# The down projection of the shared experts: one fp32 matmul on raw operands in place of three matmuls on rounded parts

## The reference

```python
def _L0_ffn_ref(x, w12, w3, router_w, expert_bias, sw1, sw2, sw3):
    g = x @ sw1.T                       # 1024 shared hidden channels
    u = x @ sw2.T
    shared_out = jax.nn.silu(g) * u @ sw3.T
    scores = jax.nn.sigmoid(x @ router_w.T)
    _, top_idx = jax.lax.top_k(scores + expert_bias, 2)     # 2 of 8 routed experts
    ...                                 # routed experts: 128 hidden channels each
    return shared_out + routed_out
```

## Time and profile before

| | us |
|---|---|
| median of 3 runs | 1803.8 (1801.58 to 1804.18) |
| the profiled execution's own time | 1802.2 |
| its span, first to last instruction | 1800.1 |
| PE busy | 1553.0 (86% of the span) |
| DVE busy | 1184.8 (66%) |
| ACT busy | 894.5 (50%) |
| mean granted TensorE clock | 0.929 of full speed |

### The profile page before, as it was taken

The page is one execution under the profiler, slowest core; times in us unless marked ns, Lnnn a source line. Parts: engine busy times, 40 slices in busy tenths (PEclk is TensorE's granted clock), DMA queues, the critical chain, the costliest instruction groups (busy, mean ns, idle before and its releaser), DMA issues. The chain is left out here.

```text
span 1800.1 us, 26927 instructions
## 1 busy us (share of the span) xinstructions
PE 1553.0 (86%) x8952; PEld 1190.4 (66%) x8958; DVE 1184.8 (66%) x2139; ACT 894.5 (50%) x2156; POOL 585.7 (33%) x688
## 2 busy tenths in 40 slices
PE   5899799889987884917699999999999999999492
PEld 4444488668863333817488888888888888888372
DVE  4666463676358996356377877778777877777632
ACT  2356444234435551415366666666666666665241
POOL 3110233312344652448322232222332223320163
PEclk9899899889987996958699999999999999999796
DMA  3320144214410005740000000000000000000463
GB/s 76 61 43 13 57 141 112 74 55 142 110 48 0 1 0 182 147 148 13 1 13 1 24 1 13 13 13 13 11 15 1 25 1 13 1 1 1 164 142 110
DMA packets 62053, 89.95 MB, mean 50 GB/s; under 512 B 10192, under 2 KB 44240, under 8 KB 61920
## 3 DMA queue, kind: packets, MB, share of 16 engines
q1 hardware_dynamic: 53664, 65.68, 11.9%
q0 software_dynamic: 8256, 22.56, 5.8%
HBM read 62.38 MB, written 19.40 MB: 45 GB/s over the span
## 5 line engine op out<-in xcount | busy, mean ns | idle before, releaser
L1375 DVE TENSOR_REDUCE gqa_neg_max<-acc 128x1 f32<-128x1024 f32 (+7 forms) x256 | 193.4, 755 | 176.4 <-PE acc L1484 175.2
L1261 ACT ACTIVATE gqa_probsT_high<-aux 128x512 fp32r<-128x512 f32 x288 | 172.0, 597 | 249.5 <-PE aux L1492 248.7
L1380 DVE TENSOR_TENSOR gqa_probsT_low<-aux,gqa_probsT_high 128x512 fp32r<-128x512 f32 x288 | 198.2, 688 | 29.8 <-ACT gqa_probsT_high L1261 25.5
L1270 ACT ACTIVATE gqa_probs<-acc,gqa_neg_max 128x1024 f32<-128x1024 f32 (+7 forms) x256 | 189.3, 739 | 31.4 <-DVE gqa_neg_max L1375 26.3
L1492 PE MATMUL aux<-ident,gqa_probs 128*128 128x128 f32 x1152 | 174.4, 274 | 0.0
L504 POOL DMA_INDIRECT f_xs<-tokens,f_slot_token x108 | 106.8, 989 | 140.8 <-DVE f_slot_token L670 84.2
L1503 PE MATMUL aux<-gqa_probsT_high,gqa_v_high 128*128 128x512 f32 x288 | 146.6, 509 | 1.0 <-DVE gqa_probsT_low L1380 1.0
L1168 POOL TENSOR_SCALAR gqa_q_scale<-gqa_q_scale 128x4 f32<-128x4 f32 x64 | 16.3, 255 | 383.3 <-ACT gqa_square L1205 383.0
L1515 PE MATMUL aux<-gqa_wo,gqa_oT 128*128 128x256 f32 x512 | 132.4, 381 | 4.4 <-DVE stream L1368 3.5
L1482 PE MATMUL acc<-gqa_k_high,gqa_q_low 128*128 128x512 f32 (+5 forms) x384 | 132.8, 346 | 0.0
L1482 PE MATMUL acc<-gqa_k_low,gqa_q_high 128*128 128x512 f32 (+5 forms) x384 | 132.7, 346 | 0.0
(11 more groups left out here) (401 smaller groups left out, 3951.4 us busy)
## 6 DMA issues: line engine op xcount, KB each, us to landing
outputs_by_slot<-f_y_tile SPq DMA_DIRECT2D x108, 128.0 KB
f_ws<-in_f_up SPq DMA_DIRECT2D x48, 256.0 KB, 4.2
f_ws<-in_f_down SPq DMA_DIRECT2D x48, 128.0 KB, 4.3
mat_qk<-mat_high SPq DMA_DIRECT2D x64, 64.0 KB, 2.3
f_w<-in_f_up SPq DMA_DIRECT2D x16, 256.0 KB, 4.4
tokens<-f_ln_xn SPq DMA_DIRECT2D x4, 1024.0 KB, 6.1
gqa_w_q<-in_g_wq SPq DMA_DIRECT2D x8, 512.0 KB, 3.5
gqa_wo<-in_g_wo SPq DMA_DIRECT2D x8, 512.0 KB, 3.8
```

The costliest lines, as they stand in the source:

```text
L1261: act.activation(probsT_high[:, u % RING, :], aux[:, u % 2, :], ACT.Copy).then_inc(cell_high_ready, 1)
L1270: act.activation(out, scores(n), ACT.Exp, bias=neg_max[:, j % (2 * JOBS):j % (2 * JOBS) + 1], accum_out=row_sum[:, n // 2 % 4, m, n % 2:n ...
L1375: dve.tensor_reduce(neg_max[:, j % (2 * JOBS):j % (2 * JOBS) + 1], scores(n), AXY, ALU.max, negate=True).then_inc(max_ready, 1)
L1380: dve.tensor_tensor(probsT_low[:, u % RING, :], aux[:, u % 2, :], probsT_high[:, u % RING, :].bitcast(F32), ALU.subtract).then_inc(cell_lo ...
```

## The change

For the shared experts the down projection uses the raw fp32 hidden values and the raw fp32 down weights. The parts `round` go away on ACT and on DVE, and with them `high`, `low` and their semaphores. `split` works on the 512 up columns only. The down weights have buffers of their own (`w_down`, four slots): those of experts 0 to 3 are loaded where they were loaded before, and those of experts 4 to 7 after all other loads in SP's list, each behind a wait for the down steps that free its slot. `down` waits for `hidden` and for its weights. `hide` waits for the down step that read its buffer, four steps earlier.

```diff
             if i == 3:
-                steps.extend([("round", 0), ("place", 0)])
+                steps.append(("place", 0))
             elif i == 4:
-                steps.extend([("invert", 0), ("round", 1), ("round", 2), ("down", 1), ("round", 3)])
-            elif i > 4 and i != FRONT:
-                steps.append(("round", i - 1))
+                steps.extend([("invert", 0), ("down", 1)])
...
-            w = sb("w", [P, STAGES, UP + D])
+            w = sb("w", [P, STAGES, UP])
+            w_down = sb("w_down", [P, SLOTS, D])
...
-            w_high = sb("w_high", [P, SLOTS, UP + D], F32R)
-            w_low = sb("w_low", [P, SLOTS, UP + D], F32R)
+            w_high = sb("w_high", [P, SLOTS, UP], F32R)
+            w_low = sb("w_low", [P, SLOTS, UP], F32R)
...
-            high = sb("high", [P, SLOTS, HALF], F32R)
-            low = sb("low", [P, SLOTS, HALF], F32R)
...
-                sp.dma_start(w[:, m % STAGES, UP:], down_dram[e:e + 1].rearrange("a p n -> (a p) n")).then_inc(w_in[m % STAGES], 16)
+                if e < SLOTS:
+                    sp.dma_start(w_down[:, e, :], down_dram[e:e + 1].rearrange("a p n -> (a p) n")).then_inc(down_in[e], 16)
+
+            for e in range(SLOTS, shared):
+                sp.wait_ge(down_done, 2 * (e - SLOTS) + 2)
+                sp.dma_start(w_down[:, e % SLOTS, :], down_dram[e:e + 1].rearrange("a p n -> (a p) n")).then_inc(down_in[e % SLOTS], 16)
...
-                act.wait_ge(w_in[m % STAGES], 32 * (m // STAGES) + 32)
+                act.wait_ge(w_in[m % STAGES], 16 * (m // STAGES) + 16)
...
                 if n >= HIDDEN:
-                    dve.wait_ge(low_ready, n - HIDDEN + 1)
+                    dve.wait_ge(down_done, n - HIDDEN + 1)
...
-                pe.wait_ge(low_ready, n + 1)
+                pe.wait_ge(hidden_ready, n + 1)
+                if n % 2 == 0:
+                    pe.wait_ge(down_in[s], 16 * (n // 2 // SLOTS) + 16)
...
-                    for a, b in three(high[:, n % SLOTS, cols], low[:, n % SLOTS, cols], w_high[:, s, UP:], w_low[:, s, UP:]):
-                        last = pe.matmul(acc[:, tile // 2, tile % 2 * D:(tile % 2 + 1) * D], a, b,
-                                         start=False, stop=False, skip_group_check=True)
+                    last = pe.matmul(acc[:, tile // 2, tile % 2 * D:(tile % 2 + 1) * D], hidden[:, n % HIDDEN, cols], w_down[:, s, :],
+                                     start=False, stop=False, skip_group_check=True)
```

More of the change, by code:

```diff
@@ L282, in sparse @@
                 steps.extend([("turn", s), ("part", s)])
-            if shared and s == 0:
-                steps.append(("round", FRONT - 1))
             if shared and s < 2:
@@ L305, in order @@
             dense(i)
-        steps.append(("round", 2 * shared - 1))
         steps.extend([("down", 2 * shared - 2), ("down", 2 * shared - 1)])
@@ L401, in ffn_layer @@
         w_in = [sem(f"w_in{r}") for r in range(STAGES)]
+        down_in = [sem(f"down_in{r}") for r in range(SLOTS)]
         w_high_ready = sem("w_high_ready")
@@ L408, in ffn_layer @@
         hidden_ready = sem("hidden_ready")
-        high_ready = sem("high_ready")
-        low_ready = sem("low_ready")
         down_done = sem("down_done")
@@ L556, in _ @@
                     silu(n)
[L557 to L561, removed]
                 elif kind == "part":
@@ L707, in _ @@
                     shares()
[L708 to L711, removed]
                 elif kind == "part" and not PLAIN:
```

## The result

The changed kernel took 1809.24 us (median of 10 runs, 1805.2 to 1813.01) against 1800.35 us (10 runs, 1795.57 to 1804.18) for the kernel before. The medians are 8.9 us apart; the ratio of the runs, which is not that of the two medians, is 1.0041, with a 95% interval of 1.0027 to 1.0055. By this interval it is slower by 4.9 to 9.9 us. The forecast was 1809.5 us, in a range of 1804 to 1815, and a difference of +6.7 us. That the time hits so closely is partly luck, since further runs of the kernel before came out lower than the three known then. A second timing gave 1.0036 (1.0022 to 1.0050), with medians 5.2 us apart.

What follows compares the result with a forecast made beforehand. PE's list of matmuls was taken to bound the two shared layers; dearer down steps +9.6, ended waits -2.2 and smaller splits -0.7 made +6.7 us, forecast 1809.5 us, range 1804 to 1815.

Steps and rivals of the forecast that it cites:

- PE is the bound: In both shared layers PE hardly pauses, so their length is PE's list of matmuls and the change is priced there.
- The price of a step: Each of 32 down steps goes from 1.42 to 1.72 us, eight fp32 records of 0.215 us: +9.6 us.
- The rule of four passes for three: At the down steps, a true fp32 product takes four passes: 1.90 us, +0.47 us a step, +15 us in all.
- The waits that go: PE's waits for rounded hidden before down(0), down(1), down(7) and down(15) end: 1.1 us a layer, -2.2 us.
- The smaller splits: Shorter splits on ACT and DVE are almost all unneeded cover: -0.7 us, bounds 0 and -1.4.
- in two places: Shorter splits reach PE only at the second layer's start, -0.3 us, and before up(2), together -0.4 us.
- What is moved: Four late down-weight loads per layer, last in SP's list, and hide's new wait for down(n-4) cost nothing.
- The sum: Whole kernel: +9.6 - 2.2 - 0.7 = +6.7 us, forecast 1809.5 us.
- The swallowing rival: PE's pauses in the shared layers vanish, gaining 6.2 us; net +3.4 us, 1805.6 to 1807.2 us; chance 0.11.
- The clock: PE's granted clock is 1.00 behind the first layer's head; falling below 1.00 there would show the prediction wrong.

Runs made afterwards that it cites:

- Doubling the step: The changed kernel with each down matmul issued twice; 1861.14 us.
- reordering: The kernel before with its three-part down step and only the order of roundings, splits and the last token tile's addition changed; ratio 0.9978, median 1798.24 us.
- The run with one part: The kernel before with only the product of the two rounded parts in down, four matmuls a step in place of twelve; 1787.6 us.
- the rounding kept: The changed kernel with the rounding kept on ACT and DVE, its results unread, and down made to wait for it; 1808.38 us.
- The run with only the matmul changed: The kernel before with down on raw operands; wide splits, rounding and waits for it stay; ratio 1.0055, median 1810.24 us.
- the run with wide splits: The changed kernel with all splits but the first widened again to 768 columns, the last 256 of them zeros; 1812.78 us.

## Why the prediction was right

*PE is the bound.* Right, within limits. Doubling the step and reordering moved the time by what PE's list says. The run with one part shows the limit: a fall of 0.95 us a step is paid out only by half.

*The price of a step.* Right in mechanism, a little high in size: 0.215 us a record, as the sparse tiles had it, but the step differs by 0.288 us and not 0.30, so +9.2 us in place of +9.6; the 0.30 came from single starts rounded against the change. The rule of four passes for three, from the Trainium skill (FP8 and Floating Point Precision, section TensorE Precision Notes), would make the ratio of the steps 1.33 if a pass cost what a part costs. No trace here agrees with that ratio: the steps stand at 1.71 / 1.42 = 1.20, and the measurement decides.

*The waits that go.* Predicted 0.33, 0.23, 0.32 and 0.24 us a layer; the gains of A, B, C and E are 0.36, 0.41, 0.31 and 0.21. Only B is clearly off. There two clearing matmuls stand ahead of `down(1)`, and the first of them waits for DVE's cast of the slots. The 0.64 us in the earlier trace rows are not that wait: the first clearing matmul has no record in that trace. The second trace of the kernel before has both, and a wait of 0.42 us. There DVE comes to the cast from a split:

```profile
249.90 0.95 DVE L586 TENSOR_TENSOR f_w_low<-f_w,f_w_high 128x768 fp32r<-128x768 f32 x1
250.76 0.17 DVE L670 CAST f_slot_token<-acc 128x23 uint32<-128x23 f32 x1
...
250.99 0.61 PE L918 MATMUL acc<-zeros 128*128 128x512 bf16 x2 [0.42 <-DVE f_slot_token L670]
```

In the changed kernel the wait is 0.28 us, since DVE is early and waits for the turn-over itself, 2.46 us:

```profile
247.73 0.18 DVE L663 CAST f_slot_token<-acc 128x23 uint32<-128x23 f32 x1 [2.46 <-PE acc L895]
...
247.97 0.60 PE L908 MATMUL acc<-zeros 128*128 128x512 bf16 x2 [0.28 <-DVE f_slot_token L663]
248.41 3.62 PE L776 MATMUL acc<-f_w_down,f_hidden 128*128 128x256 f32 x16
```

The prediction had not counted these 0.14 us; with its 0.23 they make 0.37 of the 0.41. The missing rounding is not what brings them. With the rounding kept DVE is early as well, and the second clearing matmul stands 249.94 - 249.26 = 0.68 us behind the last matmul of the turn-over, as in the changed kernel; in the kernel before it was 0.82 in both traces (in the first, 245.53 less 244.71). In the kernel before:

```profile
244.71 0.17 PE L905 MATMUL acc<-f_in_tile_start,f_in_row 128*128 128x23 bf16 x1
```

With the rounding kept (this trace lacks the record of the first clearing matmul too, so the 0.50 us are not all wait):

```profile
249.26 0.17 PE L913 MATMUL acc<-f_in_tile_start,f_in_row 128*128 128x23 bf16 x1
249.47 0.18 DVE L677 CAST f_slot_token<-acc 128x23 uint32<-128x23 f32 x1 [0.34 <-PE acc L913]
...
249.94 0.38 PE L926 MATMUL acc<-zeros 128*128 128x512 bf16 x1 [0.50 <-DVE f_slot_token L677]
```

The run with only the matmul changed has 0.67. So the longer `down(0)`, which puts the turn-over later, is what covers DVE here; the 0.26 us that the kept rounding adds in B are the wait before `down(1)` itself. For C and E the gain was right and the reason too narrow: longer steps cover these two waits even where the rounding stays.

*The smaller splits.* This is the step that failed, by its sentence that they reach PE "in two places". The term was put at 0.7 us, with a bound of 1.4; by the traces it is 2 x 0.47 + 0.3 + 0.3 = 1.5. The start of the second layer came as described: PE now waits for L601's successor, L594, and the first router matmul starts 3.18 us after the first transposes, where it took 3.51. At `up(2)` of the second layer 0.27 us went (0.91 to 0.64 from the first ranking matmul to the second matmul of `up(2)`), as priced. The second layer of the run with the rounding kept has 0.64 too, so it is the split and not the rounding. It shows only behind an early rise of the clock: where the first two up steps take 7.2 us, the distance is 0.56 us in the kernel before and in the changed one. For the 0.1 us put on the first layer the changed kernel has no trace with an early rise. The third place was missed, 0.47 us a layer at the first sparse tiles, where the splits on ACT and DVE are on PE's path. The window of 36 us averages this start, where ACT and DVE are late, with twenty tiles where they are not. The start of the second layer in the changed kernel:

```profile
405.13 0.63 ACT L518 ACTIVATE f_w_high<-f_w 128x512 fp32r<-128x512 f32 x1 [0.62 <-DMA f_w<-in_f_up]
...
406.92 0.61 PE L842 MATMUL aux<-xnT_high,f_w_router_parts 128*16 128x256 f32 x2 [0.57 <-DVE f_sum_parts L594]
```

*What is moved.* Right. SP's queue issues the four late loads between 250.33 and 269.85, and the first store after them at 275.30; no down step waited for weights.

```profile
250.33 19.52 SPq L458 DMA_DIRECT2D f_w_down<-in_f_down  x4
275.30 24.65 SPq L462 DMA_DIRECT2D outputs_by_slot<-f_y_tile  x16
```

*The sum.* Steps +9.2, gains 2 x 1.76 + 0.3 + 0.3 = 4.1: +5.1 us by the traces, where +6.7 was forecast. Two errors that add up: the steps were put 0.4 us too high and the gains 1.2 us too low. The swallowing rival counted on 6.2 us; gains of two thirds of that size came, though not all from the pauses that it named. The runs themselves say +4.9 to +9.9, and +4 to +9 in the second timing. Whether the 1 to 2 us between the traces' sum and the middle of these intervals is chance is open. The 0.9 us by which the whole layers stand further apart in the traces than that sum is mainly the clock: its late rise falls on four of six layer starts of the changed kernel and on one of four of the kernel before.

*The clock.* The prediction put 1.00 in the stretches behind the head, which held from 240 us on, and named a lower clock there as a sign of being wrong. The sign came in one stretch, with 0.85; the second trace of the kernel before has it as well (0.85 from 231.37 to 243.00 us). The prediction did not expect the granted clock to rise as late as in the changed kernel's first layer. There the first `up` matmuls of 512 columns stand 0.43 us apart (the 1.2 GHz level) and then 0.23 us (2.4 GHz):

```profile
229.10 0.63 PE L763 MATMUL aux<-xnT_low,f_w_high 128*128 128x512 f32 x1
229.53 0.63 PE L763 MATMUL aux<-xnT_high,f_w_low 128*128 128x512 f32 x1
...
232.08 0.40 PE L763 MATMUL aux<-xnT_high,f_w_low 128*128 128x512 f32 x1
232.31 0.39 PE L763 MATMUL aux<-xnT_high,f_w_high 128*128 128x512 f32 x1
```

Over all eleven traces of this study, kernels before, changed and experimental, the first two up steps took about 5.7 us nine times and 7.2 to 7.4 us thirteen times: eight of eleven in the first shared layer, five of eleven in the second. The kernel before shows both values in the first layer. So the late rise is not the changed kernel's alone. Whether it is more frequent there (three of three in the first layer, against one of two) these runs cannot tell.

## What to carry to other kernels

Price a matmul from the distance between starts of the same kind in the same kernel, not from its duration or its number of products: one fp32 product cost 1.20 times its three rounded parts here, and took the rounding of hidden off ACT and DVE and still lost. Before crediting a lighter side engine with nothing, look at the start-up of each pipeline, where the side engine's instruction stands in line ahead of the one that PE wants; a window over the whole stage hides it. And where the gain of a change is waits that end, try the order alone: here it kept the cheap matmul and got the gains too.

## What the runs showed of the hardware that was not expected

Stretches of PE that wait for nothing variable repeat to 0.02 us between executions, while whole executions of one kernel spread over 8 us and more. A part of that spread is the moment at which TensorE's clock rises after a head with pauses: the same first two up steps took 5.7 or 7.2 us. In the changed kernel's second layer the head from the first transposes to the first `up` took 9.47 us in one execution; in the run with wide splits, at the low clock all through, it took 12.67 us (a granted 0.50).
